# Delta rule with its inverse in two diagonal blocks of 64, and global and sparse attention rewritten beside it

## The reference

```python
# delta: 4 key heads, 8 value heads, 128 wide; q, k, v from a causal convolution of 4 taps
S = S * jnp.exp(gt)[..., None, None]
kv = jnp.einsum('bhk,bhkv->bhv', kt, S)
delta = (vt - kv) * bt[..., None]
S = S + jnp.einsum('bhk,bhv->bhkv', kt, delta)
o = jnp.einsum('bhk,bhkv->bhv', qt, S)
# sparse: 16 heads of 8; the scores that choose the queries
q_scores = 0.5 * l2 + 0.3 * entropy + 0.2 * var        # of Q = x @ Wq.T + bq, per head
# global: 16 query heads of 64, 4 key heads, rotary
q = q * cos + _rotate_half(q) * sin                    # halves (x1, x2) -> (-x2, x1)
attn = softmax(einsum('bhid,bhjd->bhij', q, k) * SCALE)
out = einsum('bhij,bhjd->bhid', attn, v)
```

## Time and profile before

| | us |
|---|---|
| median of 3 runs | 3885.16 (3882.11 to 3892.41) |
| the profiled execution | 3877.67, its span 3875.9 |
| mean granted clock of PE | 0.945 |

### The profile page before, as it was taken

How to read it: one execution, slowest core, us unless ns; L and a number is a source line. 1 busy time by engine, 2 the same in 40 slices (tenths; PEclk the granted TensorE clock), 3 DMA queues, 4 the chain that set the end, 5 groups by cost and what they waited for, 6 DMA issues and landing times. The chain is left out here.

```text
span 3875.9 us, 61610 instructions
## 1 busy us (share of the span) xinstructions
PE 3460.4 (89%) x23550; PEld 2161.1 (56%) x23550; DVE 2522.3 (65%) x4730; ACT 1832.9 (47%) x3269; POOL 1613.7 (42%) x1100
## 2 busy tenths in 40 slices
PE   6999999999857647999669999999999999978997
PEld 4777787878756435777523333333333333336776
DVE  4565656565655456777567777677677766757776
ACT  2344444434323124999423334333433333339997
POOL 1212121111104123666225556556655666656664
PEclk9999999999988557999879999999999999989999
DMA  2000000000010001000100000000000000010000
GB/s 94 1 1 1 1 1 1 1 1 1 1 45 9 6 0 44 2 2 2 38 0 1 1 1 1 1 1 1 1 1 1 1 1 1 1 44 2 2 2 12
DMA packets 21486, 31.46 MB, mean 8 GB/s; under 512 B 8418, under 2 KB 17932, under 8 KB 19724
## 3 DMA queue, kind: packets, MB, share of 16 engines
q1 hardware_dynamic: 21196, 27.52, 2.3%
HBM read 26.46 MB, written 1.05 MB: 7 GB/s over the span
## 5 line engine op out<-in xcount | busy, mean ns | idle before, releaser
L3027 POOL TENSOR_TENSOR global_acc_pool<-global_acc_pool,global_probs 128x1024 f32<-128x1024 f32 x320 | 776.7, 2427 | 470.6 <-ACT global_probs L2980 452.6
L2980 ACT ACTIVATE global_probs<-global_ps 128x1024 f32<-128x1024 f32 x512 | 524.7, 1025 | 883.2 <-PE global_ps L2853 856.9
L3075 DVE TENSOR_REDUCE global_part<-global_ps 128x2 f32<-128x1024 f32 x512 | 624.7, 1220 | 428.9 <-PE global_ps L2835 428.7
L2853 PE MATMUL global_ps<-global_q,global_k 64*128 64x512 f32 x2048 | 522.4, 588 | 0.0
L2864 PE MATMUL global_ps<-global_probs,global_v 128*64 128x512 f32 x2048 | 495.7, 605 | 0.0
L2835 PE MATMUL global_ps<-global_khh,global_qhh 64*128 64x512 f32 x1024 | 324.9, 631 | 35.9 <-DVE global_part L3075 33.9
L994 DVE COPY_PREDICATED delta_Y<-delta_tri,delta_ps 128x512 f32<-128x512 uint32 x192 | 140.4, 731 | 290.9 <-PE delta_ps L533 290.9
L900 POOL TENSOR_TENSOR delta_gm<-C_tile,delta_g 128x1024 f32<-128x1024 f32 x16 | 30.4, 1897 | 718.9 <-PE delta_ps L453 685.3
L2851 PE MATMUL global_ps<-global_mrow,global_first 64*128 64x512 f32 x1024 | 323.6, 629 | 0.0
L2864 PEld LDWEIGHTS global_ps<-global_probs,global_v 128*64 128x64 f32 x2048 | 124.3, 136 | 282.6 <-issue 161.4
L2835 PEld LDWEIGHTS global_ps<-global_khh,global_qhh 64*128 64x128 f32 x1024 | 97.9, 188 | 323.0 <-DVE global_part L3075 259.3
(11 more groups left out here) (587 smaller groups left out, 6862.3 us busy)
## 6 DMA issues: line engine op xcount, KB each, us to landing
delta_cw<-in_conv_taps SPq DMA_DIRECT2D x4, 1024.0 KB, 11.5
local_tab<-in_rot_tables SPq DMA_DIRECT2D x2, 2048.0 KB, 12.3
local_tab<-in_rot_tables SPq DMA_DIRECT2D x2, 1536.0 KB, 7.9
localw_wqkv<-in_L_ffn_wqkv SPq DMA_DIRECT2D x2, 768.0 KB
delta_wqkvz<-in_L_attn_a_W_qkvz SPq DMA_DIRECT2D x1, 1024.0 KB, 6.5
local_tab<-in_rot_tables SPq DMA_DIRECT2D x2, 512.0 KB, 4.2
...
```

What stands on the lines that cost most here:

```text
L2853: mm = pe.matmul(ps[:, 2 * (at % 2) + s, :], k2[own, group_of(u) % 2, P * k:P * k + P], q[own, u % 3, :], start=False, stop=True)
L2980: act.activation(probs[:, at % RING, :], ps[:, 2 * (at % 2):2 * (at % 2) + 2, :].rearrange("p b n -> p (b n)"), ACT.Exp).then_inc(S["probs ...
L3027: ins = eng.tensor_tensor(sums[:, u % 2, :], sums[:, u % 2, :], probs[:, at % RING, :], ALU.add)
L3075: dve.tensor_reduce(part[:, u % 2, r % SLOTS, :], ps[:, 5:7, :], X_AXIS, ALU.max)\
```

## The change

**Delta.** The two diagonal blocks of 64x64 of each head (rows and columns 0 to 63, and 64 to 127) are inverted side by side: each product is 64x64, block s in rows and columns `BLOCK[s]` of the array, and one step does both blocks of all 8 heads. The turn is a product with the identity instead of a transpose. Levels 0 to 4 work on the blocks (in `Yd`), and the last one joins them with one block of 64x64 off the diagonal, which DVE copies into Y; `place_blocks` copies the diagonal blocks into Y on ACT. NT, T, NTp and Yd have two buffers, by the tile's parity; PSUM banks are dealt anew. The order is new, in 20 slots: slot n does levels 2 (from its right products) to 5 of tile n-2, and levels 0, 1 and the turn of level 2 of tile n-1 between them. The copies of ACT and updates of DVE keep their number (two per step), over half the partitions each. Each product of a tile waits also for what read its PSUM bank last. In the setup two of the four taps' weights are scaled ahead of the wait for the gates' projection, the others right after it.

**Sparse.** The one-row products go; DVE adds the biases of q and v as it copies them from PSUM, and ACT squares q from SBUF. Rows are turned one group ahead, and the exponentials of a group run one group behind it.

**Global.** wqr, wkr and the second projections go. ACT copies the four 32-row parts of a projection into `swapped` with their halves exchanged and the sign turned, and DVE multiplies that by sin. POOL adds DVE's sums to its own (`merge_sums`), and `out_sums` reads one buffer. wq, wk and wv are loaded during the local stage before; wq is scaled on ACT; the tables come by blocks of 512 columns. At the start q0, k0 and k1 are projected first, and the rough rounds run by chunks of keys, between projections and values, in two pairs of banks.

```diff
@@ setup of the delta stage, DVE @@
+                    dve.wait_ge(S["conv_weights"], all_conv)
+                    for j in range(2):
+                        dve.tensor_tensor(wconv[:, j, :], wqkvz[:], cw[:, j, :], ALU.mult)
                     dve.wait_ge(S["ba_ps"], 1)
...
-        T_BANK, NTP_BANK, DELTA_BANK = (2, 6), (2, 7), (6, 1)
+        T_BANK, NTP_BANK, DELTA_BANK = 6, 4, 0
+        LAST = LEVELS - 2
+        BLOCK = (slice(0, P // 2), slice(P // 2, P))
...
-        SLOTS = range(0, TILES + 5)
+        SLOTS = range(0, TILES + 4)
...
@@ turn_Y @@
-                    for h in range(4 * s, 4 * s + 4):
-                        mm = pe.transpose(bank_heads(T_BANK[s], 1)[:, h % 4, :], Y[:, n % 2, h, :], ident)
+                    for h in range(HV):
+                        for s in range(1 if l == LAST else 2):
+                            mm = pe.matmul(blocks(T_BANK + s)[BLOCK[s], h, :], Yd[BLOCK[s], n % 2, h, :],
+                                           ident[BLOCK[s], BLOCK[s]], start=True, stop=True)
...
 # right_products
-                    for h in range(4 * s, 4 * s + 4):
-                        mm = pe.matmul(bank_heads(NTP_BANK[s], 1)[:, h % 4, :], NT[:, h, :], T[:, h, :],
-                                       start=True, stop=True)
+                    for h in range(HV):
+                        if l == LAST:
+                            mm = pe.matmul(blocks(NTP_BANK)[BLOCK[1], h, :], NT[BLOCK[0], n % 2, h, BLOCK[1]],
+                                           T[BLOCK[0], n % 2, h, :],
+                                           start=True, stop=True)
+                            continue
+                        for s in range(2):
+                            mm = pe.matmul(blocks(NTP_BANK + s)[BLOCK[s], h, :], NT[BLOCK[s], n % 2, h, BLOCK[s]],
+                                           T[BLOCK[s], n % 2, h, :], start=True, stop=True)
...
 # left_products: NTp by Yd in the same way
...
 # ACT
                 def keep_T(n, l, s):
-                    act.wait_ge(PAIRED["T_ps"][n % 2], step(n, l, s))
-                    act.activation(flat(T[:, half(s), :]), banks(T_BANK[s]), ACT.Copy).then_inc(PAIRED["T_ready"][n % 2], 1)
+                    act.wait_ge(PAIRED["T_ps"][n % 2], turned(n, l))
+                    act.activation(T[BLOCK[s], n % 2], blocks(T_BANK + s)[BLOCK[s]], ACT.Copy).then_inc(PAIRED["T_ready"][n % 2], 1)
...
+                def place_blocks(n):
...
+                    for s in range(2):
+                        ins = act.activation(Y[BLOCK[s], :, BLOCK[s]], Yd[BLOCK[s], n % 2], ACT.Copy)
+                    ins.then_inc(S["Y_placed"], 1)
...
 # DVE, update_Y
+                    if l == LAST:
+                        ins = dve.tensor_copy(Y[BLOCK[0], :, BLOCK[1]], blocks(DELTA_BANK)[BLOCK[0]])
+                    else:
+                        own = BLOCK[s]
+                        ins = dve.copy_predicated(Yd[own, n % 2], over_middle(tri[own, l + 1], HV),
+                                                  blocks(DELTA_BANK + s)[own])
...
 # sparse
-                            mm = pe.matmul(own, ones[0:1, :], bias[0:1, :], start=False, stop=True)
...
+                        dve.tensor_tensor(q_all[:, tiles, :], ps[:, Q_BANKS[g % 2], :].rearrange("p (t d) -> p t d", t=GROUP),
+                                          over_middle(bq, GROUP), ALU.add).then_inc(S["q_ready"], 1)
...
@@ global, PE @@
-                for n, sums in enumerate((acc, acc_pool)):
-                    for s, own in enumerate((UP, DOWN)):
-                        mm = pe.matmul(ps[own, 7, :], ones[:, 0:HD], sums[:, u % 2, BLK * s:BLK * s + BLK],
-                                       start=(n == 0), stop=(n == 1))
+                for s, own in enumerate((UP, DOWN)):
+                    mm = pe.matmul(ps[own, 7, :], ones[:, 0:HD], acc_pool[:, u % 2, BLK * s:BLK * s + BLK],
+                                   start=True, stop=True)
...
+                for c in range(CHUNKS):
+                    for qt in range(QT):
+                        rough_scores(pe, QT * c + qt)
...
 # global, ACT
+                def swap_halves(key):
...
+                    for a in range(4):
+                        b = a ^ 1
+                        ins = act.activation(swapped[32 * a:32 * a + 32, :], ps[32 * b:32 * b + 32, proj_bank(n), :], ACT.Copy,
+                                             scale=1.0 if a % 2 else -1.0)
+                    ins.then_inc(S["swap_ready"], 1)
...
@@ global, POOL @@
+                def merge_sums(u):
+                    pool.wait_ge(S["sum_step"], (u + 1) * len(dve_adds))
+                    pool.wait_ge(S["odd_step"], (u + 1) * (TILES - len(dve_adds)))
+                    pool.tensor_tensor(acc_pool[:, u % 2, :], acc_pool[:, u % 2, :], acc[:, u % 2, :], ALU.add)\
+                        .then_inc(S["merged"], 1)
```

1008 lines of the change are left out of this document (565 added, 443 removed).

## The result

| | before | after |
|---|---|---|
| median of the runs | 3884.3 us (4 runs, 3882.1 to 3892.4) | **3735.9 us** (4 runs, 3735.0 to 3737.8) |
| ratio, 95% interval | | 0.9615 [0.9598, 0.9632] |
| span of the profiled run | 3875.9 us | 3736.0 us |
| mean granted clock | 0.945 | 0.943 |

A forecast was written before the change was run, and what follows sets the result against it. PE was taken to bound the delta rule and global loop, chains of waits the sparse and global starts. Delta -147, sparse -40, global start -27 and loop -72 took 3877.7 to 3591.7; 7.5 higher for the median gave 3599, range 3535 to 3700.

The forecast's parts named there:

- rival A: Delta rule: the diagonal quadrants don't run side by side, 58 ns a record, 13.9 us more a slot, 3814 in all; chance 0.08.
- 3.2 us of waits a slot: Delta rule: handoffs between inversion steps stay open 0.4 to 0.8 us in five places, 3.2 us a slot.
- Sparse: Sparse stage: one-row bias products go, exponentials run group by group, DVE becomes the bound at 27.6 us; -40 us.
- The start of global: Start of global: weights loaded earlier, second key projections gone, rough rounds at DVE's 1.23 us; loop starts 27 us sooner.
- The step that failed in the delta rule: Delta rule: slot falls from 65.1 to 56 us, with ACT busy some 27 and DVE 38, neither binding; delta -147 us.
- 34.1 + 16.7 + 2.0: Delta slot, PE's work in us: 34.1 for the unchanged rest, 16.7 for inversion products, 2.0 for 20 mode switches.
- The step that failed in the loop: Global loop: PE sheds 44 us of projections and 29 of sums, ACT's and POOL's added work hidden; -72 us.
- C: Global loop: ACT's swap holds exponentials back and PE waits, 101 us, 3700 in all; chance 0.06.
- B: Delta rule: the handoffs stay open further, 4.5 us a slot more, 3669 in all; chance 0.22.
- D: Delta rule: inversion becomes latency, PE waits out all 25 us of handoffs, slot 78 us, 3946 in all, slower; chance 0.03.

## Why the prediction was half right

**What held.** The direction, and rival A's defeat: I took 29 ns for a record of a diagonal pair from column halves, and 31 was measured, with 56 where the blocks are not alternated. ACT's copies keep their 591 ns over half the partitions (the earlier trace rows had 598 for the whole). The row had not said that the order of the two quadrants in the queue decides. That 3.2 us of waits a slot came out as 3.19 is luck: the handoffs that I had priced are 1.12 of it (0.42 and 0.70), and 2.07 is the wait for the state.

**Sparse** (-40, measured -41) is right in size and wrong in its parts. I priced the rows at what they stand in the way, then let DVE become the bound, which it did: 35.5 us busy of 38. But I gave weight to the exponentials by group, and that is worth 1 us; the rows alone are worth 32, since they also slowed the products beside them. The 8 us that are left were not tried. **The start of global** (-27, measured -30) held.

**The step that failed in the delta rule** is "ACT would be busy some 27 us of it and DVE 38: neither binds". It is true of the sums of busy time and says nothing of when. POOL, which that sentence doesn't name, is busy 9.6 us of 60, and DVE's root and square wait for it, 1 to 2 us each. The slot was 59.9, not 56: of those 3.9 us 2.9 are the lock, the wait for the state behind it and the lower clock after it, as POOL's reordering shows. The last 1.0 is what is left of two misses that nearly cancel. PE's own work, start to start without waits, is 55.8 us in a slot (59.0 - 3.2), not 34.1 + 16.7 + 2.0 = 52.8: the pitch of 31 ns is 0.9 of the 3.0 more, the rest 0.7 (from start to start in a slot before, 28.8 us are the inversion, not 27.5, and 1.8 waits, not 3.5, which leaves 34.8 of 65.4), and the 22 switches 1.4 (3.4 in all, 0.15 each). Against that stands that the handoffs leave open 1.1 and not 3.2. Over 13 slots this is 50 us of the 82 missing. The other 32 were not tried and are read from the trace alone. The first W came at 145, not 134 (141 to 145 in the nine traces with this delta rule): up to there PE is busy 87 of 106 us (39 to 145) at a clock of 0.90, and I take it that few tiles are there to interleave. The last two slots took 53.0 and 46.9 us, not 47 and 42; in one of them PE waits 5.44 us for the state:

```profile
988.94 1.97 PE L538 MATMUL delta_ps<-delta_T,delta_NT 64*64 64x64 f32 x32 [5.44 <-DVE delta_state L1104]
...
1038.66 1.97 PE L656 MATMUL delta_ps<-C_tile,delta_core 128*128 128x128 f32 x8 [7.75 <-DVE delta_core L1122]
```

And the tail behind W of tile 15 grew by 7 us where I had taken off 3; PE is busy half of it, at 0.66. A deeper pipeline makes the steady part shorter and its two ends longer, and I had priced one slot of the end as a gain.

**The step that failed in the loop** is "hidden in the 857 us that ACT waits for scores" and the same for POOL's 27 of 45 us. PE's busy time did fall by 62 us (1435.0 to 1373.4; I had summed 73), and its idle time rose by 58. DVE, which the term doesn't name, is busy 109 us more: what POOL adds, and what DVE now reads from SBUF in place of PSUM, meet in the lock, and PE waits for DVE's maxima and `mrow`. That ACT's idle time in all doesn't hide an instruction that stands in its queue ahead of an exponential, the exchange behind DVE's product shows. The parts, by the runs: DVE's product from SBUF 27, the rest of the exchange 37, `mrow` behind the join 33. They don't add, as each removed wait uncovers another. The merge's 29 us of PE time were given back whole.

**The rivals.** C had the right place (the exchange on ACT) and a chance of 0.06, and was to cost 101 us by late exponentials; the exchange costs 64, and PE's waits for it are for DVE, none for an exponential. B's time, 3669, and C's, 3700, were both too low since each let only one thing go wrong, and the range's end of 3700 lay 36 us under the result. D did not come: of 25 us of handoffs 1.1 stay open. What I lacked was a rival for DVE and POOL together. The trace before had a sign of it: DVE's sums over 128x1024 in the loop, beside a busy POOL, took a mean of 1528 ns, where the square over 128x1024 in the delta rule took 1.23 us.
